# Transposed input as a second array, norm mean folded into the query weights, softmax rows scaled by the norm's factor, query products at 448 columns

## The reference, cut to what matters

```python
x = x + xattn(layernorm(x), ctx, Wq, Wkv, Wout)      # layernorm: (x - mean) / sqrt(var + 1e-5), no gain
    # q = layernorm(x) @ Wq.T ; k, v = split(ctx @ Wkv.T) ; 16 heads of 32
    # softmax(q k^T / sqrt(32), causal) @ v ; @ Wout.T
x = x + ffn(layernorm(x))                            # 8 experts, top 2, one shared expert of 1408, sigmoid gate
```

## Time and profile before

| | |
|---|---|
| median of 3 runs | 1526.69 us |
| time of the profiled execution | 1524.8 us |
| its span, first to last instruction | 1523.0 us |
| TensorE matmuls busy | 1492.7 us (98%) |
| VectorE, ScalarE, GpSimd busy | 869.7, 611.8, 580.9 us |
| mean granted TensorE clock | 0.998 |
| HBM read and written | 161.52 and 47.17 MB |

### The profile page before, as it was taken

One profiled execution on the slowest core, in us unless ns is written; L12 is line 12 of the kernel. 1 busy time (PEld: TensorE's weight loads), 2 busy tenths in 40 slices (PEclk: granted clock), 3 DMA queues, 4 the chain that ended last, 5 costly groups with the idle time before them and its releaser, 6 DMA issues.

```text
span 1523.0 us, 29819 instructions
## 1 busy us (share of the span) xinstructions
PE 1492.7 (98%) x10482; PEld 1279.4 (84%) x10482; DVE 869.7 (57%) x1490; ACT 611.8 (40%) x1836; POOL 580.9 (38%) x502
## 2 busy tenths in 40 slices
PE   6999999999999999999999999999999999999999
PEld 5788888888877899999999999887888888888887
DVE  6667677777665577877867867455223322233322
ACT  5877777777754333323333333422111111111111
POOL 3333446555553277865865965112100001000010
PEclk9999999999999999999999999999999999999999
DMA  6133354434356589877778765553303012030110
GB/s 193 56 99 99 86 106 87 87 91 99 75 128 123 104 317 340 287 245 266 274 257 275 248 217 184 203 183 103 98 27 111 28 54 70 14 111 28 58 54 28
DMA packets 98287, 209.96 MB, mean 138 GB/s; under 512 B 43184, under 2 KB 44208, under 8 KB 93456
## 3 DMA queue, kind: packets, MB, share of 16 engines
q1 hardware_dynamic: 86576, 177.37, 37.9%
q0 software_dynamic: 11616, 31.35, 7.2%
HBM read 161.52 MB, written 47.17 MB: 137 GB/s over the span
## 4 chain that ended last, share of the span: by engine, by line
PE 88%; DVE 3%; DMA 3%; ACT 2%; issue 2%; POOL 1%; SPq 0%; POOLq 0%; DVEq 0%; ACTq 0%
PE psum L802 62%; PE psum L1126 11%; PE psum L936 3%; PE psum L927 2%; PE psum L1028 2%; ACT probs L1227 2%; PE psum L955 1%; PE psum L1052 1%; PE psum L964 1%; PE psum L993 1%; PE psum L887 1%; PE psum L944 1%; DMA wj_raw<-in_w_shared 1%; PE psum L918 1%; PE psum L815 1%
## 5 line engine op out<-in xcount | busy, mean ns | idle before, releaser
L1527 POOL DMA_INDIRECT routed<-expert_out_dram,slot_b x56 | 55.6, 993 | 479.1 <-DVE slot_b L1986 289.3
L2004 DVE TENSOR_TENSOR h_s<-psum,silu_s 128x512 f32<-128x512 f32 x66 | 45.7, 692 | 299.6 <-PE psum L802 295.2
L802 PE MATMUL psum<-nT_hi,ws_hi 128*128 128x512 f32 x528 | 208.8, 396 | 2.9 <-DVE nT_lo L1927 2.6
L802 PE MATMUL psum<-nT_lo,ws_hi 128*128 128x512 f32 x528 | 208.6, 395 | 0.0
L802 PE MATMUL psum<-nT_hi,ws_lo 128*128 128x512 f32 x528 | 208.6, 395 | 0.0
L1227 ACT ACTIVATE probs<-psum,minus_max 112x112 f32<-112x112 f32 x512 | 176.2, 430 | 3.4 <-DVE minus_max L1662 3.4
L1499 POOL DMA_INDIRECT xg<-normed_dram,tile_ids x63 | 149.9, 2379 | 37.5 <-DMA tile_ids<-lists_dram 18.6
L802 PE MATMUL psum<-wj_hi,gT_hi 128*128 128x352 f32 x504 | 162.8, 323 | 0.0
L802 PE MATMUL psum<-wj_hi,gT_lo 128*128 128x352 f32 x504 | 162.3, 322 | 0.0
L802 PE MATMUL psum<-wj_lo,gT_hi 128*128 128x352 f32 x504 | 161.8, 321 | 0.0
L1227 ACT ACTIVATION_READ_ACCUMULATOR probs<-psum,minus_max 112x1 f32 x512 | 145.3, 284 | 0.0
(11 more groups left out here) (244 smaller groups left out, 3585.3 us busy)
## 6 DMA issues: line engine op xcount, KB each, us to landing
wj_raw<-in_w_experts SPq DMA_DIRECT2D x35, 1408.0 KB, 6.5
wj_raw<-in_w_experts SPq DMA_DIRECT2D x35, 768.0 KB, 5.2
wj_raw<-in_w_shared SPq DMA_DIRECT2D x22, 768.0 KB, 5.3
expert_out_dram<-y_c SPq DMA_DIRECT2D x63, 256.0 KB
base<-x_dram SPq DMA_DIRECT2D x8, 1024.0 KB, 5.9
x_in<-in_x SPq DMA_DIRECT2D x32, 224.0 KB, 4.1
x_res<-in_x SPq DMA_DIRECT2D x32, 224.0 KB, 3.1
x_dram<-x SPq DMA_DIRECT2D x32, 224.0 KB, 3.8
```

The lines of the kernel that those rows point to most:

```text
L802: mm = pe.matmul(out_ap, u, v, start=(n == 0), stop=(n == last))
L1527: pool.indirect_dma_start(out=routed[:, b % 2, c, :], out_offset=None, in_=expert_out_dram, in_offset=bass.IndirectOffsetOnAxis(ap=slot_b[ ...
L2004: dve.tensor_tensor(h_s[:, :], bank(b), silu_s[:, :], ALU.mult).then_inc(emptied_b[b], 1)
```

## The change

A second array xT is handed in: x laid out by batch as 128 partitions x 4 x 112. The subtraction of the mean moves into the weights (the mean over the input rows of Wq, taken by four float32 matmuls with a matrix of 1/512, is subtracted from Wq once at the start). The norm's factor is left out of the queries; it multiplies each row's scores as the scale of the exponential, with GpSimd computing it from var * 32 (`times` = SCALE ** -2). `norm1`, `xn1` and the transposes of stage `xT` go. ScalarE and VectorE split xT into high and low parts straight from SBUF (`xT_raw`). The queries of one block for a whole group of 448 columns are made in one bank instead of two blocks for 224. The hardware loop goes: all groups are written out.

```diff
-         (("x0", 0, 5), ("x0", 1, 4), ("k0", 0, 6), ("k0", 1, 7), ("q0", 0, 5), ("q0", 1, 4), ("x0", 2, 6), ("x0", 3, 7))]
+         (("k0", 0, 6), ("k0", 1, 7), ("q0", 0, 5), ("q0", 1, 4))]
-    TURNS += [((_j, "q", 0), -2, 5), ((_j, "k", 0), -2, 7), ((_j, "xT", 0), -TB, 6)]
+    if _j < 2:
+        TURNS += [((_j, "q0", 2 + _j), None, 6)]
+    TURNS += [((_j, "q", 0), -TB, 5), ((_j, "k", 0), -2, 7)]
...
-        xT_hi, xT_lo = sa("xT_hi", [P, KC, GT], F32R), sa("xT_lo", [P, KC, GT], F32R)
+        xT_hi1, xT_lo1 = sa("xT_hi1", [P, KC, GT], F32R), sa("xT_lo1", [P, KC, GT], F32R)
+        xT_hi, xT_lo = [n0_hi[:, :, 0:GT], xT_hi1[:, :, :]], [n0_lo[:, :, 0:GT], xT_lo1[:, :, :]]
-        xn1 = sa("xn1", [SEQ, TB, C])
+        xT_raw = sa("xT_raw", [P, TB, KC, SEQ])
+        mean_f = sa("mean_f", [P, P])
...
+            def load_xT(t):
+                if t >= TB:
+                    sp.wait_ge(S["xT_split"], t - TB + 1)
+                sp.dma_start(xT_raw[:, t % TB, :, :], xT[t]).then_inc(xT_loaded[t % TB], 16)
+
+            def load_x(t):
+                if t >= TB:
+                    sp.wait_ge(S["stats1"], t - TB + 1)
+                sp.dma_start(x_in[:, t % TB, :], x_tok[:, t, :]).then_inc(x_loaded[t % TB], 16)
...
-                    if before(g, NG - 2):
-                        sp.wait_ge(S["xn1_ready"], t + TB + 1)
-                        sp.dma_start(x_in[:, j, :],
-                                     x[bass.ds(t + 2 * TB, 1)].rearrange("a s c -> (a s) c")).then_inc(x_loaded[j], 16)
+                    if there(g, j, -2 * TB):
+                        load_xT(t + 2 * TB)
+                    if there(g, j, -TB):
+                        load_x(t + TB)
...
+            def weight_means():
+                pe.wait_ge(S["mean_step"], 1)
+                pe.wait_ge(w_loaded[1], 16)
                 for k in range(KC):
+                    mm = pe.matmul(bank(0), mean_f[:, :], wq_raw[:, k, :], start=(k == 0), stop=(k == KC - 1))
+                mm.then_inc(S["mean_step"], 1)
...
+                if is_first(g) and j < 2:
+                    pe.wait_ge(S["xT_split"], TB)
+                    queries(take(0, j, "q0", 2 + j), 0, HALVES[j], HT, GT)
+                if there(g, j, -TB):
+                    pe.wait_ge(S["xT_split"], TB * (g + 2))
+                    queries(take(g, j, "q"), g + 1, (j,), 0, GT)
...
+            def x_hi(t):
+                cols = slice(t % TB * SEQ, (t % TB + 1) * SEQ)
+                act.wait_ge(xT_loaded[t % TB], 16 * (t // TB + 1))
+                act.activation(xT_hi[t // TB % 2][:, :, cols], xT_raw[:, t % TB, :, :], ACT.Copy).then_inc(S["xT_hi_made"], 1)
...
-                                                          bias=minus_max[:, r, m:m + 1], scale=SCALE,
+                                                          bias=minus_max[:, r, m:m + 1], scale=rs1[:, j % 2, 1:2],
...
+                    if there(g, j, -TB):
+                        evacuate(g, j, "q", 0, qT[(g + 1) % 2], (j,), 0, GT)
                     if there(g, j, -2):
-                        evacuate(g, j, "q", 0, qT, HALVES[j % 2], *half_of(j))
                         evacuate(g, j, "k", 0, kT, HALVES[j % 2], *half_of(j))
-                    if there(g, j, -TB):
-                        x_hi(g, j, "xT", 0, turns.bank("xT"))
+                    if there(g, j, -2 * TB):
+                        x_hi(t + 2 * TB)
...
+            def centre(half):
+                cols = slice(half * C // 2, (half + 1) * C // 2)
+                dve.wait_ge(S["mean_step"], 2)
+                dve.tensor_tensor(wq_raw[:, :, cols], wq_raw[:, :, cols], bank(0)[:, cols].unsqueeze(1).to_broadcast([P, KC, C // 2]),
+                                  ALU.subtract).then_inc(S["wq_centred"], 1)
...
+                    dve.wait_ge(S["rstd1_made"], 2 * (t + 1))
                     dve.wait_ge(S["scores_done"], t + 1)
```

More of the change, by code:

```diff
@@ L24 @@
 TB = 4
-PEELED = 4
 GT = TB * SEQ
@@ L36 @@
 EPS = 1e-5
-MASKED = -3.0e38
+MASKED = -1.0e36
 SCALE = HD ** -0.5
@@ L79, in nth, with build_program @@
     def nth(self, g, j, stage, part=0):
-        if stage not in ("x0", "q0", "k0") and j < 0:
+        if stage not in ("k0", "q0") and j < 0:
             g, j = g - 1, j + TB
         b = self.bank(stage, part)
-        if isinstance(g, int):
-            return sum(len(self.of(i, b)) for i in range(g)) + self.of(g, b).index((j, stage, part)) + 1
-        all_of = [key for key, _, bank in TURNS if bank == b and key[0] >= 0]
-        return sum(len(self.of(i, b)) for i in range(PEELED)) + (g - PEELED) * len(all_of) + all_of.index((j, stage, part)) + 1
+        return sum(len(self.of(i, b)) for i in range(g)) + self.of(g, b).index((j, stage, part)) + 1
     def bank(self, stage, part=0):
         return next(bank for key, _, bank in TURNS if key[1:] == (stage, part))
-def build_program(nc, x, ctxT, wq, wkv, wout, gates, w_experts, w_shared, out):
+def build_program(nc, x, xT, ctxT, wq, wkv, wout, gates, w_experts, w_shared, out):
     NB = x.shape[0]
@@ L296, in build_program @@
         x_loaded = [sem(f"x_loaded{j}") for j in range(TB)]
+        xT_loaded = [sem(f"xT_loaded{j}") for j in range(TB)]
         xres_loaded = [sem(f"xres_loaded{i}") for i in range(2)]
@@ L1156, in evacuate @@
                 wait_filled(act, g, j, stage, part)
-                act.activation(dst[:, ms[0]:ms[1] + 1, at:to], bank(b, P, GT).rearrange("p (m s) -> p m s", m=2),
+                act.activation(dst[:, ms[0]:ms[-1] + 1, at:to], bank(b, P, GT).rearrange("p (m s) -> p m s", m=len(ms)),
                                ACT.Copy).then_inc(emptied[b], 1)
             def first_front():
-                for j in range(2):
-                    x_hi(0, -1, "x0", j, turns.bank("x0", j))
+                for t in range(2):
+                    x_hi(t)
                 weights_hi(0)
@@ L1170, in first_front @@
                 for i in range(2):
-                    evacuate(0, -1, "q0", i, qT, HALVES[i], 0, HT)
-                for j in range(2, 4):
-                    x_hi(0, -1, "x0", j, turns.bank("x0", j))
+                    evacuate(0, -1, "q0", i, qT[0], HALVES[i], 0, HT)
+                for t in range(TB, 2 * TB):
+                    x_hi(t)
             def fc0_high(c):
@@ L1452, in body @@
                         split_context(2 * g + 3, g + 1, 0)
-                    if before(g, NG - 1):
-                        inverse_root(mv1, rs1, j % 2, "stats1", "rstd1_made", t + TB + 1)
+                    if there(g, j, -1):
+                        scaled_root(t + 1)
                     if routes(g - 1) and before(g, NG + 1):
@@ L1584, in late_consts @@
                 dve.tensor_copy(tile_no[:, :], tile_no_i[:, :]).then_inc(S["consts_copied"], 1)
-            stats1(0, 1, 1)
-            stats1(1, 2, 1)
-            norm1(0, 1)
-            norm1(1, 2)
-            for n in range(2):
-                x_lo(0, -1, "x0", n, n)
+            x_lo(0)
+            x_lo(1)
             weights_lo(0)
+            centre(0)
+            centre(1)
             weights_lo(1)
@@ L1595, in _ @@
             mask_copies()
-            stats1(2, 3, 1)
-            stats1(3, 4, 1)
-            norm1(2, 3)
-            norm1(3, 4)
+            stats1(0)
+            x_lo(2)
+            x_lo(3)
             weights_lo(3)
-            for n in range(2, 4):
-                x_lo(0, -1, "x0", n, n)
+            for t in range(TB, 2 * TB):
+                x_lo(t)
             SLOT_STEPS = 6
@@ L1650, in step @@
                     dve.reciprocal(rinv[:, :], rsum[:, (j + 1) % 2, :]).then_inc(S["rinv_made"], 1)
-                if there(g, j, 1 - TB) and not (is_first(g) and j == 0):
-                    x_lo(g, j - 1, "xT", 0, t + TB - 1)
-                if is_first(g) and j == 0:
-                    stats1(j, t + TB + 1, g + 2)
                 if there(g, j, 0):
+                    dve.wait_ge(S["rstd1_made"], 2 * (t + 1))
                     dve.wait_ge(S["scores_done"], t + 1)
@@ L1670, in step @@
                     n0_low(3)
-                if before(g, NG - 1) and not (is_first(g) and j == 0):
-                    stats1(j, t + TB + 1, g + 2)
+                if there(g, j, -1):
+                    stats1(t + 1)
                 if not is_late(g, 0):
                     rows_copy(g, j)
-                if before(g, NG - 1):
-                    if is_first(g):
-                        wait_filled(dve, 0, -1, "x0", j)
-                    else:
-                        wait_filled(dve, g - 1, j, "xT")
-                    norm1(j, t + TB + 1)
+                if there(g, j, 1 - 2 * TB) and t:
+                    x_lo(t + 2 * TB - 1)
                 if there(g, j, 1):
```

158 lines of the change are left out of this document (72 added, 86 removed).

## The result

| | before | changed |
|---|---|---|
| median | 1527.06 us (4 runs, 1522.23 to 1528.37) | 1589.11 us (4 runs, 1586.12 to 1590.93) |
| ratio | | 1.041, 95% interval 1.0381 to 1.044 |
| profiled execution | 1524.8 us | 1586.12 us |
| TensorE matmuls busy | 1492.7 us (98%) | 1509.3 us (95%) |

The change made the kernel 62 us slower. The forecast was slower by 18, with a range that ended at 1567: the direction and the mechanism were right, the size was not.

A forecast was written before the change was run, and what follows sets the result against it. TensorE, busy 98%, was taken to bound the kernel, and a 13.25 us load loop the changed one. Terms 4.7 + 1.3 + 13 - 8 + 7 = +18 on 1524.8 gave 1542.8, as median 1545 us, range 1518 to 1567.

The forecast's parts named there:

- ScalarE's wait for `xT_raw`: ScalarE waits for the xT load some 2 us each step to t = 23; TensorE idles about 0.85 us before `outT`.
- TensorE's gain: TensorE's work per step falls from 13.0 to 12.4 us: 0.32 from the transposes, 0.29 from wide query matmuls.
- The rival that a wide matmul costs two narrow ones: Queries: one matmul of 448 columns costs two of 224, gaining 0; changes little, about 2 us; no chance given.
- the start: Before step 3: +2.5 for splitting weights and first xT, +2.2 for step 1's extra queries, sum +4.7 us.
- the length of the loop: Load, ScalarE, TensorE, residual and SyncE form a loop of 13.25 us a step, with a landing of 4.0.
- The piece from the high part to `normT`: In the loop: `x_hi` to `v_sb` 0.46, to `probsT` 0.5, four copies 1.84, last quarter of `outT` 0.3.
- the clock: TensorE stalls lower its clock: half of the nine longer stalls at 1.6 us each, +7 (0 to +34).
- rival C: Much slower: each stall of the 21 steps costs the clock, 34 in place of 7, 1572 us; chance 0.10.
- late landings: Nine of steps 12 to 23 with indirect stores cost 1.4 us more each than 13.25, 12.6 in all.
- the end: Steps 24 to 31 load no xT, so TensorE's gain counts there: -8 us (-5 to -11).
- A: Faster: ScalarE does not hold TensorE up, 21 steps give 0.6 us each, 1511 us; chance 0.12.
- B: No change: the loop holds, but indirect stores move away and no stall lowers the clock, 1525 us; chance 0.22.

The follow-up runs named there:

- e1_lead: Changed kernel with each load of xT issued one step ahead, batch t + 9 instead of t + 8: 1525.11 us, ratio 0.9985.
- e2_row: Changed kernel with the load of xT issued right after the store of x1, ahead of three other issues in SyncE's row: 1532.79 us, ratio 1.0033.
- e12_narrow: Kernel with loads one step ahead, early reciprocal and ranks behind queries, its queries again in 24 matmuls of 224 columns: 1516.6 us, ratio 0.9938.
- e4_alone: Changed kernel with the loads of x_in and context behind xT held back until xT has been split: 1571.91 us, ratio 1.029.
- e8_noind: Changed kernel without the indirect stores of token numbers, only the start of step 24 compared: 385.6 instead of 390.6 us.
- e5_rinv: Kernel with loads one step ahead, plus VectorE's reciprocal of row sums moved ahead of aT's low part and routing: 1521.24 us, ratio 0.9976.

## Why the prediction was right, and where it was wrong

**Right: the mechanism.** ScalarE's wait for `xT_raw`, forecast at some 2 us in each step and measured at 3.2, with TensorE idle behind it, is what the traces show, and taking it away (e1_lead) or shortening its loop (e2_row) gave back 64 and 56 us. TensorE's idle time lies ahead of the transposes of the probabilities, not ahead of `outT`. The rule that the prediction cited beside it from the Trainium skill, "DMA: Bandwidth & Descriptors", section "Rules for kernel authors", to issue a load early and to wait for it late, agrees: one step more of lead was worth 64 us here.

**Right: TensorE's gain.** The step of 12.4 us was forecast and 12.38 was measured where TensorE is the bound. Its two terms were 0.32 and 0.29; e12_narrow puts the second at 0.24, which leaves 0.38 for the transposes, the larger of the two values that the prediction read. The rival that a wide matmul costs two narrow ones falls with that.

**Right: the start.** +4.7 was forecast, +5.1 measured. The first exponential began at 27.91 us, near 28 as forecast.

**Wrong: the length of the loop, the step that failed.** The prediction summed 13.25 us, and the floor measured is 14.22. Three of its terms were short. The landing was taken at 4.0 from loads with nothing large behind them; xT has x_in behind it and needs 4.35 with the wake-up (e4_alone: 3.55 with nothing behind). The piece from the high part to `normT` was taken as the copies of ScalarE and a quarter of `outT`, 3.1; it is 3.48, because half of the transposes of the probabilities wait for the bank that `v_sb` empties, and the reciprocal sums and all of `outT` follow them. ScalarE's copies were read; TensorE's queue, in which the waits for banks stand, was not. And 4.14 from `normT` to the end of the addition was 4.47, mainly since VectorE began the addition 0.40 us after the last matmul instead of 0.13: it had `attnT` to do first, which waits for `rinvT` behind eight exponentials of ScalarE. The prediction allowed 0 to 0.05 us for the scale read from SBUF in each and let ScalarE's idle time cover it. It is 0.09, and behind a wait ScalarE has no idle time: the eight stand in the loop. By these rows, as an estimate, the old exponentials would have brought `rinvT` some 0.7 us sooner and left the last 0.27 us to TensorE; no run tested that. Together the loop is 0.97 us longer than summed, in 21 steps 20 us, a little under half of the 44 that were missed.

**Wrong: the clock.** Half of nine stalls were counted at 1.6 us each, +7. It was 13 of 21 steps at 1.1 to 1.4 us (one at 2.6), +18. This follows in the main from the first error: a loop of 13.25 would have left stalls of 0.85 us, and of the seven stalls of 1.1 to 1.64 us in this trace six left the clock at 1.00; with 14.22 plus late landings 14 of 21 are 1.86 us or longer. The rule cited with rival C, the Trainium skill, "Perfetto Trace Analysis", section "Matmul Optimizations", that matmuls should run back to back for the sake of the engine's power, is borne out in part: by it alone all 21 stalls would have cost the clock, and 13 did.

**Half right: late landings.** +12.6 was forecast for steps 12 to 23, all of it put on the indirect stores. Measured were +11.5 there, of which some 6 us are the stores' (e8_noind), and +5.4 in steps 3 to 11, where none was forecast; that the sum comes near is luck in part. Steps 8 and 9, ahead of the first of these stores, have landings of 5.76 and 5.38 us. The context's load, issued right behind the row in every fourth step, may be one cause: in e8_noind the five loads with the context behind them land after 4.9 to 6.5 us, the other sixteen, but for one of 5.25, after 3.5 to 5.0. No run took the context's load away by itself, and what delays the others isn't settled.

**Wrong: the end.** -8 forecast, -1.4 measured. The steps without loads did shrink, but step 24 still pays for the last stalled load, and behind short idle times in 480 to 484 us the clock fell once more:

```profile
480.00:484.00 4.00, 2.95 (x19) 0.94 0.08 23
484.00:488.00 4.00, 4.00 (x53) 0.50 0.72 197
```

**The rivals.** A would have needed no wait on ScalarE. Its price, 1511, was also too good: even with the wait taken away the kernel ran at 1525, since the work that a 13 us step had covered (the late reciprocal, the ranks) came due. B and C are both refuted: the loop was longer than B's, and C's clock fell in 13 steps and not in all. That C's 1572 is the nearest of the numbers says nothing for it, since its loop was 13.25 too.

## What to carry to other kernels

When a DMA's issue depends on a step's result and its landing is waited for in the same step, the DMA is a link in the step's loop: add up the whole loop, with every wait for a bank on the engine behind it and with every path that joins it again, before trusting a small margin. The cheap cure is distance: the load has four buffers here, and issuing it one step earlier was worth more than any order of the queues that was tried. And a step that is made shorter uncovers the waits that it had hidden; here three edits were needed until 0.6 us less on TensorE showed in the time.

## What the runs showed of the hardware that was not expected

- The length of one idle time does not decide whether the granted clock falls. In the changed kernel stalls of 1.55, 1.86 and 1.89 us were followed by 0.50, stalls of 1.91 and 2.69 us were not, nor was one of 2.67 us in e4_alone. In e5_rinv, of the four longer idle times ahead of the rank matmuls, one of 1.67 and one of 0.88 us were followed by 0.50, another of 1.67 and one of 1.95 were not. And at 484 us it fell behind idle times of 0.56, 0.21 and 0.28 us. What decides it is open.
- A fall costs 1.1 to 1.4 us here (once 2.6), for about 3 us at the low level, because the chain behind the stall is TensorE's own: `sumT`, `outT`, `normT` and the projection.
- A load of 224 KB landed 3.5 us after its issue with nothing issued behind it, and 4.4 with another of the same size behind it (e4_alone, the changed kernel): what is issued later slowed what was under way. In e2_row it landed after 3.2 to 4.4 us with four transfers behind it, but with one ahead of it instead of four; how much each neighbour costs isn't shown.
- An exponential of 112x112 whose scale is read from SBUF takes 0.42 us from one to the next, with a constant scale 0.33.
